# Linear attention on one Trainium2 core: another order of each engine's work within a step, and two places for clearing semaphores instead of seven

## The reference, cut to what matters

```
x = layernorm(X)
K = x.reshape(B, L, H, d)
Q = rms_norm_multihead((x @ Wq.T).reshape(B, L, H, d), q_norm_w)
V = rms_norm_multihead((x @ Wv.T).reshape(B, L, H, d), v_norm_w)
W = cumsum(einsum('blhd,blhe->blhde', K, V), axis=1)
X = X + einsum('blhd,blhde->blhe', Q, W).reshape(B, L, D)
# then, for the 16 experts: layernorm of X, logits, the two largest, softmax
```

## Time and profile before

| | |
|---|---|
| three executions | 4502.37, 4509.51, 4507.91 us, median 4507.91 us |
| profiled execution, its own time | 4506.27 us |
| its span, first to last instruction | 4504.5 us |
| TensorE, busy share of the span | 88% |
| VectorE | 79% |
| ScalarE | 59% |
| GpSimd | 49% |
| mean granted TensorE clock | 0.931 of full |

### The profile page before, as it was taken

The page is one execution under the profiler, slowest core; times in us unless marked ns, Lnnn a source line. Parts: engine busy times, 40 slices in busy tenths (PEclk is TensorE's granted clock), DMA queues, the critical chain, the costliest instruction groups (busy, mean ns, idle before and its releaser), DMA issues. The chain is left out here.

```text
span 4504.5 us, 54711 instructions
## 1 busy us (share of the span) xinstructions
PE 3984.1 (88%) x17866; PEld 3005.5 (67%) x17866; DVE 3574.9 (79%) x4436; ACT 2646.0 (59%) x3555; POOL 2209.0 (49%) x1837
## 2 busy tenths in 40 slices
PE   6774998683999999999999999999999999989563
PEld 3443554452788888888888888888888888867421
DVE  4454443774899999999999999999999999956611
ACT  4442333331677777777777777777777777742221
POOL 1234665464455555555555555555555555530154
PEclk8776999786999999999999999999999999989776
DMA  6001333666222232223222322232223223137296
GB/s 242 20 22 39 56 61 59 221 217 185 63 53 57 49 81 50 57 49 81 53 53 49 81 55 53 57 76 56 51 58 72 56 51 64 34 113 235 74 243 165
DMA packets 349678, 384.04 MB, mean 85 GB/s; under 512 B 141532, under 2 KB 279585, under 8 KB 336851
## 3 DMA queue, kind: packets, MB, share of 16 engines
q1 hardware_dynamic: 325334, 354.22, 30.8%
q0 software_dynamic: 24064, 26.32, 3.5%
HBM read 232.55 MB, written 117.84 MB: 78 GB/s over the span
## 5 line engine op out<-in xcount | busy, mean ns | idle before, releaser
L1523 POOL TENSOR_TENSOR at_pl<-at_pf,at_ph 128x512 fp32r<-128x512 f32 x1024 | 1330.0, 1299 | 1343.0 <-ACT at_ph L1670 1342.7
L1669 ACT ACTIVATE at_pf<-at_ps_s 128x1024 f32<-128x1024 f32 x1024 | 1051.0, 1026 | 747.5 <-PE at_ps_s L1719 747.5
L1586 DVE TENSOR_TENSOR at_pl<-at_pf,at_ph 128x512 fp32r<-128x512 f32 x1024 | 1355.4, 1324 | 20.6 <-ACT at_ph L1670 20.6
L1568 DVE TENSOR_REDUCE at_mx<-at_ps_u 128x2 f32<-128x1024 f32 x1024 | 1250.2, 1221 | 24.5 <-PE at_ps_u L1703 24.4
L1670 ACT ACTIVATE at_ph<-at_ps_s 128x1024 fp32r<-128x1024 f32 x1024 | 1042.7, 1018 | 0.0
L1719 PE MATMUL at_ps_s<-at_q,at_k 66*128 66x512 f32 x2048 | 820.7, 401 | 0.0
L1718 PE MATMUL at_ps_s<-at_q,at_k 128*128 128x512 f32 x2048 | 812.2, 397 | 0.3 <-ACT at_ph L1670 0.3
L1735 PE MATMUL at_ps_v<-at_ph,at_vh 128*128 128x512 f32 x2048 | 810.1, 396 | 0.2 <-POOL at_pl L1523 0.2
L1737 PE MATMUL at_ps_v<-at_pl,at_vh 128*128 128x512 f32 x2048 | 809.5, 395 | 0.0
L1736 PE MATMUL at_ps_v<-at_ph,at_vl 128*128 128x512 f32 x2048 | 809.2, 395 | 0.0
L1703 PE MATMUL at_ps_u<-at_k,at_qp 128*128 128x512 f32 x2048 | 648.0, 398 | 63.5 <-DMA at_q<-at_low 47.7
(11 more groups left out here) (254 smaller groups left out, 4116.1 us busy)
## 6 DMA issues: line engine op xcount, KB each, us to landing
at_k<-kT SPq DMA_DIRECT2D x64, 512.0 KB, 10.0
at_q<-qT SPq DMA_DIRECT2D x64, 512.0 KB, 9.3
wgu<-Wgu_in SPq DMA_DIRECT2D x64, 384.0 KB, 5.2
qT<-pj_rot SPq DMA_DIRECT2D x32, 512.0 KB, 3.1
vT<-pj_vo SPq DMA_DIRECT2D x32, 512.0 KB, 4.4
kT<-pj_rot SPq DMA_DIRECT2D x32, 512.0 KB, 3.1
at_raw<-qT SPq DMA_DIRECT2D x32, 512.0 KB, 4.7
at_raw<-kT SPq DMA_DIRECT2D x32, 512.0 KB, 6.6
```

The costliest lines, as they stand in the source:

```text
L1523: pool.tensor_tensor(pl[:, n % NP, at], pf[:, n % NP, at], ph[:, n % NP, at].bitcast(F32), ALU.subtract).then_inc(s["pl2_ready"], 1)
L1568: dve.tensor_reduce(mx[:, qb % 2, 2 * i:2 * i + 2], ps_u[:], X, ALU.max).then_inc(s["u_max"], 1)
L1586: dve.tensor_tensor(pl[:, n % NP, at], pf[:, n % NP, at], ph[:, n % NP, at].bitcast(F32), ALU.subtract)\
L1669: act.activation(pf[:, n % NP], ps_s[:, n % 2], ACT.Exp, scale=DH ** -0.5)
```

## The change

What it does, in seven parts:

1. **TensorE**: logits and positions move from the head of a step to a place between outputs_T and scores.
2. **VectorE**: squares_sum and roots move ahead of logits, counted and masked; the second measure moves ahead of them all.
3. **ScalarE**: tokens moves ahead of roots, roots ahead of outputs, and routed_T goes last, behind routed.
4. **ScalarE**, smaller: the two copies into `qf` with a scale become one of 256 columns without; the scale moves into a mask `blocksw` that VectorE makes once and multiplies `kvm` by.
5. **The biases** load behind the norms' weights, ahead of the tiles of x from the second DMA on; the split comes at step -7, and its result is stored ahead of the zeros.
6. **The last four routed tiles** alternate between `ps_t` and the now idle `ps_qv`, so two can be under way.
7. **Semaphores** are cleared behind `project` and at the end of the program, and not at the end of each stage.

```
@@ build / scope @@
             self.project()
+            self.release()
             self.softmax_attention()
...
             self.add_odd()
+            self.release()
...
-        def release():
-
-            nc.clear_and_free_semaphores(held)
-            nc.all_engine_barrier()
-        ctx.callback(release)
+    def release(self):
+
+        self.nc.clear_and_free_semaphores(self.held)
+        self.nc.all_engine_barrier()
+        self.held = []
@@ SyncE @@
                 sp.dma_start(normw[:], ins["qvw"]).then_inc(s["norms"], 16)
+                sp.dma_start(bsrc[:, 0:2 * F0], ins["bgu"]).then_inc(s["biases"], 16)
+                sp.dma_start(bsrc[:, 2 * F0:], ins["bd"]).then_inc(s["biases"], 16)
                 for q in range(1, Q):
                     load_x(q)
...
+                sp.wait_ge(s["bias_split"], 5)
+                sp.dma_start(self.bias_dram[:].rearrange("k e n -> e k n"), bpart).then_inc(s["bias_out"], 16)
                 sp.wait_ge(s["zero_ready"], 1)
@@ VectorE @@
-                        dve.tensor_tensor(dst, ps_k[:, 1], blocks.unsqueeze(1).broadcast_to([P, DC, P]), ALU.mult)\
+                        dve.tensor_tensor(dst, ps_k[:, 1], blocksw[:], ALU.mult)\
...
+                        link(dve.tensor_tensor(blocksw[:], blocks.unsqueeze(1).broadcast_to([P, DC, P]),
+                                               normw[:, :, 0:1].broadcast_to([P, DC, P]), ALU.mult))
+                    if i == -7:
+                        split_biases()
+                    if i == -1:
+                        dve.wait_ge(s["bias_out"], 16)
@@ ScalarE @@
-                        m = act.activation(qf[:, t % 3, c], src, ACT.Copy, scale=normw[:, c, 0:1])
-                    m.then_inc(s["q_ready"], 1)
+                    act.activation(qf[:, t % 3], ps_t[:, 1].rearrange("p (c l) -> p c l", c=DC), ACT.Copy).then_inc(s["q_ready"], 1)
...
                         squares(i + 4)
+                    if tile(i + 6):
+                        tokens(i + 6)
+                    if tile(i + 4):
+                        roots(i + 4)
                     if tile(i):
                         outputs(i)
-                    if tile(i - 7):
-                        routed_T(i - 7)
...
                         routed(i - 6)
+                    if tile(i - 7):
+                        routed_T(i - 7)
@@ TensorE @@
-                    if tile(j):
-                        if i > 0:
-                            pe.wait_ge(s["xa_ready"], min(i, NT))
...
-                        logits(j)
...
                         outputs_T(i)
+                    if tile(j):
+                        if i > 0:
+                            pe.wait_ge(s["xa_ready"], min(i, NT))
...
+                        logits(j)
...
                     if tile(i + 1):
                         scores(i + 1)
```

More of the change, by code:

```diff
@@ L220, in linear_attention @@
             pq = sb("pq", [P, DC, 2])
+            blocksw = sb("blocksw", [P, DC, P])
             stats = sb("stats", [P, 2, 2, 6])
@@ L298, in sums, with routed_at @@
                 return (TB - 2) * (t // TB) + max(0, min(t % TB, LAST) - 1)
+            def routed_at(t):
+                return ps_qv[:, 0:D] if t >= NT - 4 and t % 2 else ps_t[:, 0]
             vn3 = vn[:].rearrange("p r g t d -> p r (g t d)")
@@ L523, in _ @@
                     j = i - 8
-                    if tile(j) and j % 4 == 3:
-                        logits(j // 4)
-                    if tile(j - 1) and (j - 1) % 4 == 3:
-                        counted((j - 1) // 4)
                     if i == FIRST:
@@ L534, in _ @@
                                           normw[:, :, 0:1].broadcast_to([P, DC, 2]), ALU.mult).then_inc(s["pq_ready"], 1)
-                    if tile(i + 1):
-                        masked(i + 1)
-                    if tile(i + 4):
-                        squares_sum(i + 4)
-                    if tile(i):
-                        update(i)
-                        measure(i, (s["xa_ready"], i + 1), mv2, s["mv2_ready"])
-                    if tile(i + 4):
-                        roots(i + 4)
+                        link(dve.tensor_tensor(blocksw[:], blocks.unsqueeze(1).broadcast_to([P, DC, P]),
[4 more added lines that the diff above has]
+                        dve.wait_ge(s["bias_out"], 16)
                     t = i + 12
@@ L546, in _ @@
                         measure(t, (s[f"x{t // 4}"], 16), mv1, s["mv1_ready"])
+                    if tile(i + 4):
+                        squares_sum(i + 4)
+                        roots(i + 4)
+                    if tile(j) and j % 4 == 3:
+                        logits(j // 4)
+                    if tile(j - 1) and (j - 1) % 4 == 3:
+                        counted((j - 1) // 4)
+                    if tile(i + 1):
+                        masked(i + 1)
+                    if tile(i):
+                        update(i)
+                    if tile(i):
+                        measure(i, (s["xa_ready"], i + 1), mv2, s["mv2_ready"])
                     t = i + 10
@@ L674, in _ @@
                         squares(i + 4)
+                    if tile(i + 6):
+                        tokens(i + 6)
+                    if tile(i + 4):
+                        roots(i + 4)
                     if tile(i):
                         outputs(i)
-                    if tile(i - 7):
-                        routed_T(i - 7)
-                    if tile(i + 4):
-                        roots(i + 4)
-                    if tile(i + 6):
-                        tokens(i + 6)
                     if tile(i + 11) and (i + 11) % 4 == 3 and i + 11 > 3:
```

49 lines of the change are left out of this document (23 added, 26 removed).

## The result

The changed kernel takes **4380.26 us** (median of four executions, 4378.60 to 4382.21) against 4506.09 us of the kernel before, measured beside it on the same chip (4502.37 to 4509.51): a ratio of 0.9724, 95% interval 0.9712 to 0.9737. The forecast was 4399 with a range from 4384; the gain is 126 us where 109 were forecast. A second and a third measurement of the changed kernel gave 4377.93 and 4371.73 us.

The account below looks back on a forecast made before the run. A ring of waits between TensorE and VectorE in linear attention was taken as the bound. Start, tiles, tail and releases summed to -109 us on the profiled 4506.27, 4397; forecast for the median 4399, range 4384 to 4440.

Parts of the forecast that it names:

- The step with the change: Linear attention, one tile's step laid out from the opening transposition at full clock; taken as 8.2 us a step.
- TensorE's own work: Linear attention step: TensorE's operations from the opening transposition to the end of the update, 8.1 us, set the step.
- The ring through the state: Linear attention: masks, product, GpSimd's addition, state matmuls, masked part, logits and scores close in 7.0 us, slack 1.1.
- Start: Up to tile 0 of linear attention: tokens no longer wait behind masks, sum and root, so openings come sooner; -5.2 us.
- Tiles 27 to 31: Last linear attention tiles, without projection: 25.6 us against 28.6, a gain of 3.0 us.
- Tail: End of linear attention: GpSimd's last scatters no longer wait for the biases' split; -4.9 us.
- Releases: Ends of stages: five semaphore clearings go at 0.5 us each, -2.5 us, between -1.5 and -4.
- The new wait: Rival: ScalarE's close or the reciprocal ahead of the masks comes a microsecond late; step 9.2, 4426 us, chance 0.17.
- ScalarE's close: ScalarE's last operation in a step, the routed tile's copy, ends at +7.85 us; slack 0.25, the thinnest.
- The second rival: The ring stays: masks wait behind ScalarE's root, step as long as the old one; 4495 us, chance 0.04.
- The clock rival: Linear attention at 1.2 GHz throughout: TensorE alone sets the step, about +4 us a tile; 4610 us, chance 0.02.
- The second rule: VectorE operations with two SBUF inputs, or a cast, and GpSimd operations lock each other out; some 0.3 us every fourth step.

Follow-up runs that it names:

- early2: The changed kernel with VectorE's product of the update moved from behind the next tile's four masks to between the second and third: 4362.07 us, ratio 0.9682.
- after_third: The changed kernel, unchanged, measured a third time, beside the kernel before with 16 added transpositions a step: 4371.73 us, ratio 0.9698.
- tail_warm: The changed kernel with 12 transpositions of the identity matrix behind the updates of tiles 27 to 30: 4375.91 us, ratio 0.9712.
- pe_order_alone: The kernel before with TensorE's new order only, logits and counting behind the masked part: 4490.26 us, ratio 0.9965.
- dve_order_undone: The changed kernel with VectorE's loop back in its former order, masks first and reciprocal last: 4522.53 us, ratio 1.0047.

## Why the prediction was wrong, and where it was right

**The step that failed** is the first of "The step with the change": "All offsets are from the opening transposition (250.72), at full clock", and with it "So TensorE's own work is 8.1 us". The 3.4 us for the projection in it were measured at 1.2 GHz (clock 0.51 in 251.19 to 254.62), while the forecast was for 2.4 GHz. It takes 1.88 us there. TensorE's own work in a plain step is 7.10 - 0.55 = 6.55 us, not 8.1. The sign stood in the earlier trace rows: a mean clock of 0.79 between the levels 1 and 0.5 says that two fifths of the time are at half speed, and TensorE's longest piece, close behind its standstill, is where to look. The prediction did take the new clock as 1.00, and it quoted the Trainium skill, TensorE: Matmul & The Clock Gate (Part 1), for it; the trace agrees (1.00 over 189 us). It then failed to apply the same clock to its own durations. The range had a bound from above (8.9 a step) and next to nothing below 8.1, so it could not take this in.

**The ring through the state** was found and priced right: 7.0 forecast, 7.11 measured. It was set aside as having 1.1 us of slack against 8.1. With 8.1 corrected to 6.55 it is the bound, and `early2` shows it by shortening it. Without logits the ring is 0.55 us shorter, 6.55, which by chance is also the figure of TensorE's own work with them. Putting 7.1 and, for tiles without logits, 6.55 in place of 8.2 and 7.35 gives for tiles 7 to 27 20 x 7.1 = 142 (measured 144.4; the steps around a choice add 0.5 per four, 0.4 forecast) and for tiles 0 to 7 7 x 6.55 = 45.9 (measured 45.0).

**Start**: -8.1 against -5.2. Profiles of kernels with the changed kernel's start have tile 0 between 37.3 and 39.7 us, those with the start of the kernel before between 47.7 and 50.4, so the gain there is 8 us or more. The forecast drew its 5.2 from the tokens and the roots. The runs with ScalarE's or VectorE's order taken back don't bear this out: tile 0 comes at 40.6 and 40.4 in them. Which of the edits gives the gain stays open.

**Tiles 27 to 31**: 34.10 in the first profile, 27.43 in `after_third`, 25.6 forecast. The forecast is near where no stalls of the `remote` kind fall in. Part of what is left may again be the clock: without projections TensorE idles more in these steps, and the clock is 0.88 there. In a group with stalls it was 0.72, and `tail_warm`, which raised it, gave back 4.6 us.

**Tail**: 54.22 in the first profile, 49.00 in `after_third`, 46.9 forecast. The biases' wait went, as said. GpSimd still pauses for the last choice (3.43 us in `after_third`), which the forecast had left out.

**Releases**: 2.5 us forecast, none found; so small a gain would not show in the times. The later stages' difference lies within what profiles of kernels with the same later stages differ by.

**The rivals.** The new wait did not come: ScalarE's close held its place. It comes if ScalarE keeps its old order (8.34 a step). The second rival, a step as long as the old one, comes with TensorE's order alone (`pe_order_alone`), though by another wait: for ScalarE's tokens, not for VectorE's masks. The clock rival lay the wrong way round: with the standstill gone the clock rose. Its price of 4610 isn't what its terms give either (27 x 4 on 4508 is 4616), which changes nothing. In `dve_order_undone` the orders bring standstills of 3.7 us back, and the clock of 0.80 lengthens the step in turn: its projection takes 3.27 us. How much of the 12.77 is the one and how much the other was not taken apart. The second rule that was quoted, of the Trainium skill, SBUF — State Buffer (Who interferes with whom), had the addition of 16 columns as its witness (391 ns). The trace of before bears it out for this operation. Four of the eight take 0.60 to 0.62 us; each ran while GpSimd was at a multiplication (`normed`) and ended within 0.02 us of the end of one (181.62 against 181.61, for one). The other four had no GpSimd operation beside them and took 0.17. In the changed kernel none of the eight has one beside it, and all take 0.17. So the change took this waiting away, where the prediction expected more of it. The section is narrower than the prediction told it: GpSimd's operation has to read SBUF, and a cast only can take the shared ports.

## What to carry to other kernels

Before a duration of TensorE goes into a sum, read the granted clock of exactly its stretch: a piece that stands behind a standstill may be at half speed, and closing the standstill then shortens the piece too. Work the second-longest ring out as carefully as the longest, since any error in the first makes it the bound. Orders on several engines that form one ring are one change: TensorE's alone gave 17 us, the whole change without VectorE's order cost 20, and the whole change gave 126.

## What the runs showed of the hardware

- Sixteen useless transpositions a step made the kernel before 28 us faster. In the step of the earlier trace rows, after a standstill of 2.75 us at a clock of 1.00, the clock was at 0.50 for the projection and at 1.00 again behind it; over the 239 us of tiles 7 to 27 its mean was 0.79. In the changed kernel, with standstills of 0.55 us in steps of 7.1, it stayed at 1.00. The Trainium skill, TensorE: Matmul & The Clock Gate (HAM oscillation — how this bites in real kernels), describes such a rising and falling between bursts and says to restructure so that TensorE stays busy. The trace agrees in the direction.
- In some groups what waits for TensorE starts late while GpSimd issues indirect DMAs back to back (1.29 us each): 7.73 us of waiting where the same kernel has 1.21 in another group. The profile names them `remote`. Two profiles of one kernel differed by 11.9 us in the last stretches of a stage of 317, so a second one, taken at another time or on another chip, belongs beside the first before a stretch is explained. What causes them stays open.
- An addition of 16 columns on VectorE takes 0.17 us, and 0.6 where a GpSimd multiplication is under way; it then ends together with it.
- The same semaphores were cleared in seven operations in 1.71 us and in two in 1.53.
